# Attention probabilities turned in 32x32 blocks and exchanged between partitions by DMA, with one float32 product per key tile

## The chip, the core and the metric

The kernel runs on one core of one Trainium2 chip. The core has five engines that take their instructions in order and meet at semaphores: TensorE (PE, with its weight loads as PEld), VectorE (DVE), ScalarE (ACT), GpSimd (POOL) and SyncE (SP, which only issues transfers here). A row ending in q (ACTq, SPq) is an instruction of an engine's queue, such as the issue of a transfer. Data lies in SBUF (128 partitions) and in PSUM (8 banks of 2 KB per partition). The metric is the device time of one execution, in microseconds; smaller is better.

## The reference

One gated cross-attention block and one gated feed-forward block, in float32. What the change touches is the attention: 16 heads, 2 batches of 512 query rows, 1024 keys of width 128.

```python
q_big = jnp.einsum('bshk,hkq->bshq', q_hk, w_kc_q)
q_r = jnp.einsum('bshq,hqr->bhsr', q_big, W_qr)
k_r = jnp.einsum('bld,hdr->bhlr', kv_rope, W_kr)
scores = jnp.einsum('bhsr,bhlr->bhsl', q_r, k_r)
attn = jax.nn.softmax(scores, axis=-1)
ctx_c = jnp.einsum('bhsl,bld->bhsd', attn, kv_rope)
...
out = ctx_lat.reshape(b, s, H * K) @ Wo.T
...
x = x + jnp.tanh(g_xattn[0]) * _L0_xattn_ref(...)
x = x + jnp.tanh(g_ffn[0]) * _L0_ffn_ref(...)
```

## The kernel before

**Units.** The heads go in 8 pairs. A pair has 4 units `w` = 0 to 3: batch `w // 2`, and of it one half of the query rows. A unit is 4 score tiles (2 groups of 128 rows times 2 heads) of 128 rows by 1024 keys, so there are 32 units. Pair 0 is written out, pairs 1 to 3 are a loop, pairs 4 to 6 and 7 are written out again. Each unit has 8 steps `c`, one for each tile of 128 keys; tables such as `SCORE_STEP`, `MAX_STEP`, `EXP_STEP` and `SIDE` say at which step each engine does what.

**Softmax of a unit.** `score_matmuls` (L1324) makes 2 tiles in 12 products of float32 split in a high and a low part (`q_hi`, `q_lo`, `k_hi`, `k_lo`), into the 4 banks of `ps_s`. They hold 2 tiles, so each group of 12 waits until the exponentials of the 2 tiles before it are done (`exp_done`). `max_tile` (DVE, L1675) takes the row maximum, `exp_tile` (ACT, L1514) writes the exponentials to `E` with their row sums, `inv_tile` (DVE, L1680) inverts the sums, and `pool_scale` (POOL, L1128) scales the tile in place. All this is done one unit ahead of the unit whose probabilities are used.

**Probabilities times keys.** At each step TensorE turns four 128x128 pieces of `E` against the identity (L1377) into a bank of `ps_b`. ACT rounds the bank to its high part `et_hi` (L1471), DVE subtracts to get the low part `et_lo` (L1636), and `pv_matmuls` adds three products (L1335 to L1337) to `ps_ctx`, some steps behind (`PV_STEP`). When a unit's 8 key tiles are in, `ctx_high` and `ctx_low` split `ps_ctx` for the output products.

**Side tasks.** The `SIDE` table puts other products between these: `m` and `a` (weight products for the next pair, L1255 and L1266), `q` and `k` (next queries and keys, L1297 to L1299 and L1276 to L1278), `b` (L1303) and `out` (L1231 to L1233). ACT makes the high part of `a`, `q`, `k`, `b` (`side_high`) and DVE the low part, or adds an `out` to `x_sb` (`side_low`, L1661). Each result is taken out of its bank one step behind its product. The banks of `ps_b` rotate through turned probabilities and side tasks.

**Feed-forward weights.** During pairs 0 to 3 ACT sums the absolute weights in halves of 1024 columns (`sum_half`, L1528), during pairs 4 to 6 it takes their tanh (`tanh_half`, L1538) and DVE rounds them (`round_half`, L1697). SP loads each half in `sp_pair` (L1100). The feed-forward block starts during the last pair and then has the core to itself.

Of the kernel before, what the change touches and what calls it, by code (L numbers as in the profile page):

```python
# [33 lines left out]
P = 128  # L34
# [38 lines left out]
SUM_STEPS = {0: (5, 7), 1: (5,), 2: (5, 7), 3: (6,)}  # L73
TANH_STEPS = {w: (2, 6) for w in range(4)}
ROUND_STEPS = {w: (5, 7) for w in range(4)}
SUM_HALVES, QUANT_HALVES, SUM_PAIRS = 6, 8, 4
LAST_ROUND_AT = (0, 3)

SIDE = [
# [4 lines left out]
]  # L88
WK_AT = (1, 1)
KV1_AT = (1, 6)  # L90

XN_AT = ((0, 2), (0, 6), (1, 2), (1, 6))

XN_LOW_AT = ((1, 1), (1, 3), (2, 1), (2, 3))
# [3 lines left out]
def side_tasks(w, first, last):  # L98


    def wanted(task):
        before = task[:2] == ("out", 3)
        behind = task[0] in ("m", "a", "k", "q")
        return not (first and before or last and behind)
    early = last and w == 3
    return {c - early: task for c, task in SIDE[w].items() if wanted(task)}
# [50 lines left out]
BANKS = 3  # L157
PLACES = 51


def bank_users(first, last):

    users = []
    for w in range(4):
        side = side_tasks(w, first, last)
        for c in range(LT):
            users.append(("turn", w, c))
            if c in side:
                users.append(side[c])
    return users  # L170


USERS = {v: bank_users(v == "first", v == "last") for v in ("first", "mid", "last")}
PLACE0 = {"first": PLACES - 1 - len(USERS["first"]), "mid": 0, "last": 0}
PLACE = {v: {u: PLACE0[v] + i for i, u in enumerate(us)} for v, us in USERS.items()}
assert len(USERS["mid"]) <= PLACES and USERS["first"][-3:] == USERS["mid"][-3:]


def bank_of(variant, user):
    return PLACE[variant][user] % BANKS  # L180


def bank_before(variant, user):

    at = PLACE[variant][user] - BANKS
    if at < PLACE0[variant]:
        if variant == "first":
            return None, False
        at += PLACES
        mid = USERS["mid"]  # L190
        return (mid[at], True) if at < len(mid) else (None, False)
    return USERS[variant][at - PLACE0[variant]], False

def build(nc, A):
    with ExitStack() as ctx:
# [21 lines left out]
        E = sb("E", [P, 2, ST, LCTX])  # L220
# [44 lines left out]
        wq_s = sa("wq_s", [P, 2, DIM])  # L265
        wkcq_s = sa("wkcq_s", [P, 2, QT, HK])
# [10 lines left out]
        kv_hi = sa("kv_hi", [P, BATCH, LT, DC], F32R)  # L277
        kv_lo = sa("kv_lo", [P, BATCH, LT, DC], F32R)
        et_hi = sa("et_hi", [P, ET_RING, NF], F32R)
        et_lo = sa("et_lo", [P, ET_RING, NF], F32R)  # L280
        ctx_hi = sa("ctx_hi", [P, 2, SEQ], F32R)
        ctx_lo = sa("ctx_lo", [P, 2, SEQ], F32R)
# [3 lines left out]
        wo_s = sa("wo_s", [P, 2, DIM])  # L286
# [31 lines left out]
        g3 = E[:, 0, 0:2, :].rearrange("p a b -> p (a b)")  # L318
# [5 lines left out]
        ps_et, ps_side = ps_b[:, 0:2, :], ps_b[:, 2, :]  # L324
        ps_s4 = ps_s[:, :, :].rearrange("p a (b c) -> p (a b) c", c=NF)
# [7 lines left out]
        xn = E[:, 1, :, :].rearrange("p a b -> p (a b)").rearrange("p (t d) -> p t d", d=DIM)  # L333
# [39 lines left out]
        LAST_SIDE = SIDE_PER_PAIR * 7 + SIDE_BASE + len(ORDER["last"])  # L373


        def rope_parts(eng, b, ls):
# [6 lines left out]
            def table(c, lo, hi):  # L383
# [7 lines left out]
                    lambda: eng.tensor_tensor(kv_raw[:, b, ls, :], kv_raw[:, b, ls, :], rot[:, b, ls, :], ALU.add))  # L391
# [82 lines left out]
        def ffn_sp(sp):  # L474

            sp.wait_ge(et_done, LT * (UNITS - 3) + 1)
# [3 lines left out]
            sp.wait_ge(et_done, LT * (UNITS - 1))  # L480
# [593 lines left out]

        def sp_pair(sp, p, variant, mode):
            if is0(p):
                load_bw(sp, p)
            if variant != "last":

                sp.wait_ge(side_done, 2 if is0(p) else SIDE_PER_PAIR * p + (SIDE_BASE - SIDE_PER_PAIR + ORDER["mid"][("a",)] + 1))  # L1080
                load_q(sp, p + 1)
                load_wq(sp, p + 1)

                sp.wait_ge(wk_ready, p + 1)
                load_kr(sp, p + 1)
            if not is0(p):

                sp.wait_ge(side_done, SIDE_PER_PAIR * p + (SIDE_BASE - SIDE_PER_PAIR + ORDER["mid"][("b", 1)] + 1))
                load_bw(sp, p)
            if mode is None:  # L1090
                return
            if is0(p):
                for ready in (kv0_front, kv0_back, kv1_ready):
                    sp.wait_ge(ready, 1)
            for g in range(SUM_HALVES if mode == "sum" else QUANT_HALVES):
                if not (is0(p) and g < 2):
                    sp.wait_ge(w_taken, halves_before(p, mode) + (g - 1))
                j, half = divmod(g, 2)
                row = p + WPARTS * j if mode == "sum" else WPARTS * p + (j - WPARTS * SUM_PAIRS)
                sp.dma_start(w_stage[:, half, :], A["wffn"][bass.ds(row, 1), :, half * WHALF:(half + 1) * WHALF]  # L1100
                             .rearrange("o p f -> p (o f)")).then_inc(ld_w[half], 16)

        @block.sync
        def _(sp):
# [7 lines left out]
            sp.wait_ge(ld_ctx[1], 16)  # L1112
            sp_pair(sp, 0, "first", "sum")
# [27 lines left out]
        def pool_unit(pool, p, w, last=False):  # L1141

# [743 lines left out]
```

## Time and profile before

| | |
|---|---|
| median of 3 runs | 730.16 us (729.91 to 730.49) |
| span of the profiled execution | 728.8 us |
| median less the span, what lies around the profiled instructions | 1.4 us |
| 32 units of attention, from the first step to the last product on `ps_ctx` | about 37.6 to 635.5 us of the span |
| one pair of heads in the loop | 75.0 us |
| busy in the 75 us from 186 to 261 | PE 75.0, DVE 55.8, ACT 48.6, POOL 18.1 us |
| granted TensorE clock | 1.00 throughout (2.4 GHz) |

The shares of busy time tell which engine has no room left; the start times of neighbouring rows tell how long a step holds an engine, which for TensorE is shorter than the duration of one product, because products overlap. Both are used below.

### The profile page before, as it was taken

The numbers are of one execution on the slowest core, as the hardware profiler recorded it, in microseconds if no ns is written. First come the engines' busy times: TensorE is split into PE (matmuls) and PEld (weight loads), VectorE is DVE, ScalarE is ACT, GpSimd is POOL, SyncE is SP. The second block draws the span as 40 slices with busy tenths as digits, with TensorE's granted clock in tenths as the row PEclk, the third lists the DMA queues.
The fourth block names the chain that finished last, engine by engine and source line by source line (L and its number), as shares of the span: only waits on it lengthen the run. The fifth ranks groups of instructions, "written<-read, shape, count | busy, mean of one in ns | idle before, by whom it ended". The sixth has DMA issues, their size and how long they took to land.

```text
span 728.8 us, 11950 instructions
## 1 busy us (share of the span) xinstructions
PE 714.5 (98%) x4142; PEld 530.5 (73%) x4142; DVE 567.6 (78%) x1016; ACT 486.6 (67%) x821; POOL 253.2 (35%) x235
## 2 busy tenths in 40 slices
PE   9899999999999999999999999999999999999997
PEld 7577788777877787778777877787777776645553
DVE  6778877777787777767878787878887889999873
ACT  3677765666667656666666666666676766478876
POOL 4744422222212222222222223222322334677651
PEclk9999999999999999999999999999999999999999
DMA  8401164114010401040114213543250001000001
GB/s 280 149 31 58 36 240 157 46 34 154 29 58 29 158 29 58 29 158 31 59 58 158 58 59 119 178 151 117 66 191 12 28 2 58 1 1 28 17 30 45
DMA packets 22124, 58.32 MB, mean 80 GB/s; under 512 B 4032, under 2 KB 7232, under 8 KB 21312
## 3 DMA queue, kind: packets, MB, share of 16 engines
q1 hardware_dynamic: 19904, 44.96, 18.5%
q0 software_dynamic: 784, 10.49, 3.8%
q10 hardware_dynamic: 1392, 2.29, 0.9%
q8 instruction: 26, 0.43, 0.2%
q14 instruction: 18, 0.15, 0.1%
HBM read 51.45 MB, written 6.29 MB: 79 GB/s over the span
## 4 chain that ended last, share of the span: by engine, by line
PE 82%; DVE 7%; ACT 3%; POOL 3%; issue 2%; DMA 2%; ACTq 0%; SPq 0%; POOLq 0%; DVEq 0%
PE ps_b L1377 14%; PE ps_s L1324 13%; PE ps_ctx L1335 9%; PE ps_ctx L1337 7%; PE ps_ctx L1336 7%; PE ps_s L587 4%; PE ps_b L1233 4%; PE ps_b L1231 4%; PE ps_b L1232 4%; PE ps_b L1297 2%; PE ps_b L638 2%; PE ps_b L1299 2%; PE ps_b L1298 2%; PE ps_b L1266 2%; PE ps_b L1303 2%
## 5 line engine op out<-in xcount | busy, mean ns | idle before, releaser
L1128 POOL TENSOR_SCALAR E<-E,small 128x1024 f32<-128x1024 f32 x128 | 148.7, 1162 | 413.0 <-DVE small L1680 413.0
L1471 ACT ACTIVATE et_hi<-ps_b 128x512 fp32r<-128x512 f32 x256 | 152.9, 603 | 163.1 <-PE ps_b L1377 163.1
L1636 DVE TENSOR_TENSOR et_lo<-ps_b,et_hi 128x512 fp32r<-128x512 f32 x256 | 175.0, 684 | 43.0 <-ACT et_hi L1471 42.4
L1675 DVE TENSOR_REDUCE small<-ps_s 128x1 f32<-128x1024 f32 x128 | 153.0, 1216 | 4.7 <-PE ps_s L1324 3.0
L1377 PEld LDWEIGHTS ps_b<-ident,E 128*128 128x128 f32 x1024 | 124.7, 140 | 40.6 <-issue 8.8
L1377 PE MATMUL ps_b<-ident,E 128*128 128x128 f32 x1024 | 152.1, 273 | 1.3 <-DVE et_lo L1636 0.8
L1514 ACT ACTIVATE E<-ps_s,small 128x1024 f32<-128x1024 f32 x128 | 142.9, 1117 | 5.7 <-DVE small L1675 5.5
L1335 PE MATMUL ps_ctx<-et_hi,kv_hi 128*128 128x512 f32 x256 | 121.0, 472 | 0.7 <-DVE ctx_lo L1636 0.7
L1337 PE MATMUL ps_ctx<-et_lo,kv_hi 128*128 128x512 f32 x256 | 101.1, 395 | 0.0
L1336 PE MATMUL ps_ctx<-et_hi,kv_lo 128*128 128x512 f32 x256 | 100.5, 393 | 0.0
L1661 DVE SCALAR_TENSOR_TENSOR x_sb<-ps_b,small,x_sb 128x512 f32<-128x512 f32 x62 | 46.2, 746 | 29.3 <-PE ps_b L1233 29.3
L1335 PEld LDWEIGHTS ps_ctx<-et_hi,kv_hi 128*128 128x128 f32 x256 | 48.3, 189 | 25.1 <-issue 15.6
L1324 PE MATMUL ps_s<-k_hi,q_hi 64*128 64x512 f32 x256 | 57.2, 443 | 3.1 <-ACT E L1514 1.5
L587 PE MATMUL ps_s<-wq,q12T 128*128 128x512 fp8e4 x256 | 59.9, 379 | 0.1
L1337 PEld LDWEIGHTS ps_ctx<-et_lo,kv_hi 128*128 128x128 f32 x256 | 48.0, 188 | 11.1
L1324 PE MATMUL ps_s<-k_hi,q_lo 64*128 64x512 f32 x256 | 50.8, 391 | 0.0
L1324 PE MATMUL ps_s<-k_lo,q_hi 64*128 64x512 f32 x256 | 50.6, 390 | 0.0
L1231 PE MATMUL ps_b<-b_hi,ctx_hi 128*128 128x512 f32 x128 | 50.4, 394 | 0.0
L1233 PE MATMUL ps_b<-b_lo,ctx_hi 128*128 128x512 f32 x128 | 50.3, 393 | 0.0
L1336 PEld LDWEIGHTS ps_ctx<-et_hi,kv_lo 128*128 128x128 f32 x256 | 48.8, 191 | 1.5
L1232 PE MATMUL ps_b<-b_hi,ctx_lo 128*128 128x512 f32 x128 | 49.8, 389 | 0.0
L514 POOL TENSOR_TENSOR hg<-h_f,E 128x512 f32<-128x512 f32 x32 | 40.5, 1276 | 21.2 <-DVE h_f L922 21.2
(188 smaller groups left out, 1070.0 us busy)
## 6 DMA issues: line engine op xcount, KB each, us to landing
w_stage<-in_wffn SPq DMA_DIRECT2D x48, 512.0 KB, 3.4
xnT<-xn_split POOLq DMA_DIRECT2D x3, 2048.0 KB, 9.5
wo_s<-in_woT SPq DMA_DIRECT2D x8, 512.0 KB, 6.0
xn_split<-xnT POOLq DMA_DIRECT2D x2, 2048.0 KB, 9.3
wq_s<-in_wq SPq DMA_DIRECT2D x7, 512.0 KB, 5.8
wkcq_s<-in_wkcqT SPq DMA_DIRECT2D x7, 384.0 KB, 4.3
out<-x_sb SPq DMA_DIRECT2D x8, 256.0 KB, 2.0
x_sb<-in_x SPq DMA_DIRECT2D x3, 512.0 KB, 7.3
```

Of the source, the lines that this page charges most:

```text
L587: last = nc.tensor.matmul(ps_s4[:, 2 * i + c % 2, :], q12T[:, k, i, d, :], wq8[:, DT * i + d, cols], start=(d == 0), stop=(d == DT - 1))
L1128: nc.gpsimd.tensor_scalar(e, e, rowinv[:, k:k + 1], 1.0, ALU.mult, ALU.mult).then_inc(scaled, 1)
L1231: nc.tensor.matmul(into, ctx_hi[:, u % 2, cols], b_hi[:, h, :], start=(h == 0), stop=False)
L1324: last = nc.tensor.matmul(ps_s[:, h, cols], q[head, b, rows], k[head, b, cols], start=(i == 0), stop=(i == 2))
L1335: nc.tensor.matmul(ps_ctx[:, :], kv_hi[:, b, c, :], et_hi[:, c % ET_RING, :], start=(c == 0), stop=False)
L1336: nc.tensor.matmul(ps_ctx[:, :], kv_lo[:, b, c, :], et_hi[:, c % ET_RING, :], start=False, stop=False)
L1337: nc.tensor.matmul(ps_ctx[:, :], kv_hi[:, b, c, :], et_lo[:, c % ET_RING, :], start=False, stop=(c == LT - 1))\
L1377: last = nc.tensor.transpose(into[:, s * P:(s + 1) * P], E[:, w % 2, s, c * P:(c + 1) * P], ident[:, :])
L1471: return nc.scalar.activation(out, in_, ACT.Copy)
L1514: nc.scalar.activation(E[:, w % 2, t, :], ps_s[:, t % 2, :], ACT.Exp, bias=negmax[:, k:k + 1], accum_out=rowsum[:, k:k + 1]).then_inc(exp_ ...
L1636: return nc.vector.tensor_tensor(out, full, hi.bitcast(F32), ALU.subtract)
L1675: nc.vector.tensor_reduce(negmax[:, k:k + 1], ps_s[:, t % 2, :], AX_X, ALU.max, negate=True).then_inc(max_done, 1)
```

## The change

The turn of the probabilities leaves TensorE. `E` is laid out as partition, parity of the unit, key quarter, tile, 256 keys. After scaling, DVE turns each tile in place in 32x32 blocks (`turn_blocks`, 4 instructions a unit). Then 16 transfers of 32 partitions x 4 KB a unit move partition quarter `i` of `E` to quarter `g` of a new tensor `G` (`exchange`): SP issues quarters 0 and 1, ACT quarters 2 and 3, 8 transfers each. The copies `et_hi`, `et_lo`, `kv_hi`, `kv_lo` are gone, and each key tile takes one product of unsplit float32 operands, `kv` and `G`. Softmax runs two units ahead in place of one (`AHEAD = 2`), `ps_ctx` and the third bank of `ps_b` take turns as the sum of a unit, and the side tasks take turns in the other two banks. SP's loads are mixed with its exchanges. The tables of steps change accordingly.

```diff
+AHEAD = 2
+SCORE_STEP = {0: 0, 4: 1}
+MAX_STEP = {1: (0, 1), 5: (2, 3)}
+EXP_STEP = {1: 0, 2: 1, 5: 2, 6: 3}
+INV_STEP = {3: 0, 4: 1, 6: 2, 7: 3}
+TURN_OWN = {4: 0, 5: 1}
+TURN_NEXT = (2, 3)
+CTX_HIGH_STEP, CTX_LOW_STEP = 0, 1
+EXCHANGE_ACT_STEP = 1
...
+        SP_QUARTERS, ACT_QUARTERS = (0, 1), (2, 3)
...
+        def exchange(eng, passed, p, w, quarters):
+            par = w % 2
+            eng.wait_ge(blocks_turned, 16 * p + (4 * w + 4))
+            eng.sem_inc(passed, 1)
+            if not (is0(p) and w < 2):
+                eng.wait_ge(pv_done, 4 * p + (w - 1))
+            for i in quarters:
+                for g in range(4):
+                    eng.dma_start(G[g * QUAD:(g + 1) * QUAD, par, i, :, :], E[i * QUAD:(i + 1) * QUAD, par, g, :, :])\
+                        .then_inc(exchanged[par], 16)
...
+        def pv_matmul(pe, p, w, c):
+            if c == 0:
+                pe.wait_ge(exchanged[w % 2], 2 * EXCHANGE * p + EXCHANGE * (w // 2 + 1))
+                if not (is0(p) and w < 2):
+                    pe.wait_ge(ctx_done, 4 * p + (w - 1))
+            turned = G[:, w % 2, :, :, key_tile(c)].rearrange("p i t q -> p t i q")
+            last = nc.tensor.matmul(CTX_PS[w % 2].rearrange("p (t i q) -> p t i q", t=ST, i=4), kv[:, w // 2, c, :], turned,
+                                    start=(c == 0), stop=(c == LT - 1))
...
+        def turn_blocks(dve, p, w, t):
+            dve.wait_ge(scaled, 16 * p + (4 * w + t + 1))
+            nc.vector.transpose(e_tile(w % 2, t), e_tile(w % 2, t)).then_inc(blocks_turned, 1)
...
-                    act.wait_ge(et_done, 32 * p + (8 * w + c + 1))
-                    copy_act(et_hi[:, c % ET_RING, :], ps_b[:, bank_of(variant, ("turn", w, c)), :]).then_inc(ethi_done, 1)
-                    if c in EXP_STEP and not (variant == "last" and w == 3):
-                        exp_tile(act, *next_unit(p, w), EXP_STEP[c])
+                        side_high(act, p, variant, task, ps_b[:, side_bank(variant, task), :])
+                    if c in EXP_STEP and not (variant == "last" and w >= AHEAD):
+                        exp_tile(act, *unit_ahead(p, w, AHEAD), EXP_STEP[c])
+                    if c == EXCHANGE_ACT_STEP and not (variant == "last" and w == 3):
+                        exchange(act, act_passed, *unit_ahead(p, w, 1), ACT_QUARTERS)
```

ACT, the first steps of unit 0 of a loop pair, before. `et_hi` is the high part of a turned key tile, `E` gets the exponentials of a tile.

```order
L1471 ACTIVATE et_hi<-ps_b 128x512 [waits et_done]
L1512 ISA
L1514 ACTIVATE E,small<-ps_s,small 128x1024 [waits max_done]
L1552 REGISTER_ALU
L1471 ACTIVATE et_hi<-ps_b 128x512 [waits et_done]
L1512 REGISTER_ALU
L1514 ACTIVATE E,small<-ps_s,small 128x1024 [waits max_done]
L1518 ISA
L1471 ACTIVATE ctx_hi<-ps_ctx 128x512 [waits pv_done]
```

ACT, unit 1 of a loop pair, changed.

```order
L1446 ACTIVATE ctx_hi<-ps_ctx 128x512 [waits pv_done]
L1451 REGISTER_ALU
L1446 ACTIVATE b_hi<-ps_b 128x512 [waits side_done]
L1451 REGISTER_ALU
L1446 ACTIVATE k_hi<-ps_b 128x512 [waits side_done]
L1479 REGISTER_ALU
L1483 ACTIVATE E,small<-ps_s,small 128x2x4x128 [waits exchanged1,max_done]
L1055 DMA G<-E 32x1024 [waits blocks_turned,pv_done]
L1055 DMA G<-E 32x1024 x7
L1451 REGISTER_ALU
L1446 ACTIVATE k_hi<-ps_b 128x512 [waits side_done]
L1483 ACTIVATE E,small<-ps_s,small 128x2x4x128 [waits max_done]
```

Eight issues of the exchange now stand between the first exponential of a unit and the second, and in unit 1 also ahead of the second `k_hi`; before, a copy of 128x512 stood there.

DVE, the start of the same unit, changed.

```order
L1653 STREAM_TRANSPOSE E<-E 128x4x256 [waits scaled] x2
L1614 REGISTER_ALU
L1608 TENSOR_TENSOR b_lo<-ps_b,b_hi 128x512 [waits side_hi]
L1656 ISA
L1608 TENSOR_TENSOR ctx_lo<-ps_ctx,ctx_hi 128x512 [waits ctxhi_done]
L1614 REGISTER_ALU
L1608 TENSOR_TENSOR k_lo<-ps_b,k_hi 128x512 [waits side_hi]
L1641 REGISTER_ALU
L1643 TENSOR_REDUCE small<-ps_s 128x1 [waits scores_done]
L1641 REGISTER_ALU
L1643 TENSOR_REDUCE small<-ps_s 128x1 [waits scores_done]
```

The first maximum of a unit comes behind two block turns, `ctx_lo` and the low part of the side task of step 0.

PE, from step 3 to step 4 of unit 1, changed.

```order
L1333 MATMUL ps_b<-G,kv 128x512
L1340 REGISTER_ALU
L1228 MATMUL ps_b<-b_hi,ctx_hi 128x512 [waits ctx_done,side_freed]
L1229 MATMUL ps_b<-b_hi,ctx_lo 128x512
L1230 MATMUL ps_b<-b_lo,ctx_hi 128x512
L1228 MATMUL ps_b<-b_hi,ctx_hi 128x512
L1229 MATMUL ps_b<-b_hi,ctx_lo 128x512
L1230 MATMUL ps_b<-b_lo,ctx_hi 128x512
L1313 REGISTER_ALU
L1321 MATMUL ps_s<-k_hi,q_hi 128x512 [waits exp_done]
```

The second group of scores of a unit stands behind the `out` of step 3, whose wait on `side_freed` is for the side task two places back, in unit 1 the second `k`; it waits itself for the second exponential of the same unit. Before, a unit's two groups stood at steps 7 and 3, among key tiles of four transposes each.

## Rows read from the trace of the kernel before

**Rows 1.** The page: busy time, and slices of the span with the clock.

```profile
PE 714.5 (98%) x4142; PEld 530.5 (73%) x4142; DVE 567.6 (78%) x1016; ACT 486.6 (67%) x821; POOL 253.2 (35%) x235
...
PEclk9999999999999999999999999999999999999999
```

**Rows 2.** Stretches: length, PE, PEld, DVE, ACT, POOL busy, clock, DMA, GB/s.

```profile
37.00:111.00 74.00, 72.75 (x427) 55.88 (x424) 56.10 (x89) 52.51 (x94) 29.65 (x22) 1.00 0.27 93
186.00:261.00 75.00, 75.00 (x439) 58.99 (x438) 55.77 (x89) 48.58 (x90) 18.07 (x16) 1.00 0.21 67
562.00:638.00 76.00, 72.49 (x409) 53.07 (x408) 68.36 (x154) 48.68 (x82) 33.38 (x34) 1.00 0.06 21
```

**Rows 3.** PE in time: start us, us, what; one key tile.

```profile
331.72 0.60 PE L1377 MATMUL ps_b<-ident,E 128*128 128x128 f32 x4
332.07 0.48 PE L1335 MATMUL ps_ctx<-et_hi,kv_hi 128*128 128x512 f32 x1
332.38 0.40 PE L1336 MATMUL ps_ctx<-et_hi,kv_lo 128*128 128x512 f32 x1
332.62 0.39 PE L1337 MATMUL ps_ctx<-et_lo,kv_hi 128*128 128x512 f32 x1
332.85 0.60 PE L1377 MATMUL ps_b<-ident,E 128*128 128x128 f32 x4
```

**Rows 4.** PE in time: a float32 product of 512 columns, in two records.

```profile
50.07 1.02 PE L1303 MATMUL ps_b<-wo_s,wkv_s 128*128 128x512 f32 x2
50.92 0.60 PE L1377 MATMUL ps_b<-ident,E 128*128 128x128 f32 x4
```

**Rows 5.** All engines in time: one group of 12 score products, and the maxima behind it.

```profile
313.88 0.50 PE L1324 MATMUL ps_s<-k_hi,q_hi 64*128 64x512 f32 x2
...
315.47 0.50 PE L1335 MATMUL ps_ctx<-et_hi,kv_hi 128*128 128x512 f32 x1
315.57 2.36 DVE L1675 TENSOR_REDUCE small<-ps_s 128x1 f32<-128x1024 f32 x2 [0.27 <-PE ps_s L1324]
```

**Rows 6.** Groups: line, engine, what, count, busy us, mean ns, idle before.

```profile
L1636 DVE TENSOR_TENSOR et_lo<-ps_b,et_hi 128x512 fp32r<-128x512 f32 x256 | 175.0, 684 | 43.0 <-ACT et_hi L1471 42.4
L1675 DVE TENSOR_REDUCE small<-ps_s 128x1 f32<-128x1024 f32 x128 | 153.0, 1216 | 4.7 <-PE ps_s L1324 3.0
L1471 ACT ACTIVATE et_hi<-ps_b 128x512 fp32r<-128x512 f32 x256 | 152.9, 603 | 163.1 <-PE ps_b L1377 163.1
L1514 ACT ACTIVATE E<-ps_s,small 128x1024 f32<-128x1024 f32 x128 | 142.9, 1117 | 5.7 <-DVE small L1675 5.5
L1128 POOL TENSOR_SCALAR E<-E,small 128x1024 f32<-128x1024 f32 x128 | 148.7, 1162 | 413.0 <-DVE small L1680 413.0
L1697 DVE TENSOR_SCALAR wq<-w_stage 128x1024 fp8e4<-128x1024 f32 x24 | 16.3, 678 | 0.0
L390 POOL TENSOR_TENSOR wq<-wq,w_stage 128x1024 f32<-128x1024 f32 x1 | 2.1, 2138 | 0.0
```

**Rows 7.** ACT's queue in time: the transfers that it issues at the start.

```profile
1.68 0.45 ACTq L1062 DMA_DIRECT2D wkcq_s<-in_wkcqT  x1
2.16 0.45 ACTq L1063 DMA_DIRECT2D wqr_s<-in_wqr  x1
2.64 1.24 ACTq L1069 DMA_DIRECT2D wkr_s<-in_wkr  x1
3.92 0.50 ACTq L1058 DMA_DIRECT2D x_sb<-in_x  x1
```

**Rows 8.** Transfers: what, issuer, count, KB each, us from issue to landing.

```profile
w_stage<-in_wffn SPq DMA_DIRECT2D x48, 512.0 KB, 3.4
xn_split<-xnT POOLq DMA_DIRECT2D x2, 2048.0 KB, 9.3
```

**Rows 9.** PE in time: the longest wait of the prologue.

```profile
19.83 0.51 PE L1324 MATMUL ps_s<-k_hi,q_hi 64*128 64x512 f32 x2 [1.51 <-DVE q_lo L1636]
```

More of the change, by code:

```diff
@@ L104, in wanted @@
         return not (first and before or last and behind)
-    early = last and w == 3
-    return {c - early: task for c, task in SIDE[w].items() if wanted(task)}
+    return {c: task for c, task in SIDE[w].items() if wanted(task)}
 PROLOGUE_TASKS = [("m",), ("a",), ("k", 0, 0), ("k", 0, 1), ("q", 0, 0), ("q", 0, 1), ("k", 1, 0), ("k", 1, 1), ("q", 1)]
@@ L152, in hi_index, with side_bank @@
     return HI_PER_PAIR * p + (HI_BASE + HI_ORDER[variant][task])
[L157 to L192, printed above, removed]
+def side_bank(variant, task):
+    return (SIDE_BASE + ORDER[variant][task]) % 2
+assert SIDE_PER_PAIR % 2 == 0
 def build(nc, A):
@@ L265, in build @@
         wq_s = sa("wq_s", [P, 2, DIM])
+        with ExitStack() as place:
+            wo_s = place.enter_context(nc.sbuf_tensor("wo_s", [P, 2, DIM], F32))
         wkcq_s = sa("wkcq_s", [P, 2, QT, HK])
@@ L1173, in pool_pair @@
                     load_xn(pool, p, 0)
+                if last and w == 2:
+                    rms_root(pool, 0)
+                    pool.wait_ge(ld_g, 32)
+                    normed(pool, -2, 0)
+                    normed(pool, -1, 1)
+                    ln2_root(pool, 1)
+                    rms_root(pool, 1)
         @block.gpsimd
@@ L1215, in _ @@
             normed_row(7)
-            for t in range(ST):
-                pool_scale(pool, 0, 0, t)
+            for w in range(AHEAD):
+                for t in range(ST):
+                    pool_scale(pool, 0, w, t)
             pool_pair(pool, 0)
@@ L1375, in pe_pair @@
-                    into = ps_b[:, bank_of(variant, ("turn", w, c)), :]
-                    for s in range(ST):
-                        last = nc.tensor.transpose(into[:, s * P:(s + 1) * P],
-                                                   E[:, w % 2, s, c * P:(c + 1) * P], ident[:, :])
-                    last.then_inc(et_done, 1)
-                    ahead, half = SCORE_STEP.get(c, (4, 0))
-                    if w + ahead < (4 if variant == "last" else 6) and ahead < 4:
-                        if (w + ahead, half) == (2, 0) and not is0(p):
+                        pe.wait_ge(xnt_copied, TT)
@@ L1387, in pe_pair @@
-                    for back, tile in PV_STEP[c]:
-                        if not (variant == "first" and w < back):
-                            pv_matmuls(pe, *((p, w - back) if w >= back else (p - 1, 3)), tile)
+                        score_matmuls(pe, *unit_ahead(p, w, AHEAD), SCORE_STEP[c])
+                    pv_matmul(pe, p, w, c)
                     if c in tasks:
                         wait_bank(pe, p, variant, tasks[c])
-                        side_matmuls(pe, p, variant, tasks[c], ps_b[:, bank_of(variant, tasks[c]), :])
+                        if mean and tasks[c] == ("out", 3, 0):
+                            pe.wait_ge(mean_chain, 1)
+                        side_matmuls(pe, p, variant, tasks[c], ps_b[:, side_bank(variant, tasks[c]), :])
@@ L1464, in _ @@
             pe_pair(pe, 7, "last")
-            for back, tile in PV_STEP[0] + PV_STEP[1]:
-                pv_matmuls(pe, 7, 3, tile)
             ffn_pe(pe)
```

352 lines of the change are left out of this document (166 added, 186 removed), and 7 rows, old and new, of the table SIDE.

## The prediction

> **What bounds the kernel now.** The page's first section comes first: TensorE is busy for 714.5 of 728.8 us, with its clock at the full level in every slice [rows 1]. The stretches show the same inside the loop: 75.0 of 75 us on PE, 55.8 on DVE, 48.6 on ACT, 18.1 on POOL [rows 2]. So the loop runs at TensorE's pace, and what takes time off TensorE pays only until something else is late. Durations of single products overlap, so I count by start times. A key tile costs four transposes 0.35 us (331.72 to 332.07) and three products 0.78 us (to 332.85), together 1.13 us [rows 3]. A group of 12 score products holds PE for 1.59 us (313.88 to 315.47), and the maxima start 1.69 us after its start [rows 5]. By the 0.23 us step of split products [rows 3] the six of an `out` take 1.4 us and the twelve of a `q` 2.8 us. A pair then is 32 x 1.13 = 36.2 us of key tiles and 36.9 us of scores and side tasks, 73.1 against the 75.0 measured; the 2 us missing are small gaps, and I add them to each pair below.
>
> **What TensorE gains.** The float32 product that takes the place of seven instructions is in the trace: it holds PE from 50.07 to 50.92, 0.85 us [rows 4]. That is 0.28 us less a tile, 9 us a pair: 64.1 + 2 = 66 us of TensorE work. The trace shows no product whose moving operand comes in runs of 32 numbers; I take the dense price, since nothing here points to another, with 0.78 us (three split steps) below and twice 0.85 above.
>
> **What the others gain and get.** ACT loses 256 copies of 0.60 us, DVE 256 subtractions of 0.68 us [rows 6], 4.8 and 5.5 us a unit. DVE gets four block turns of 128x1024 a unit. None is in the trace; the nearest rows of that size are the rounding (0.68 us, SBUF to SBUF), the maximum (1.22 us) and POOL's product of two operands (2.14 us) [rows 6]. I take 1.2, the row of DVE that moves one number a lane in a step, with 0.68 and 2.14 for the range. DVE's sum stays near 53 us a pair, ACT's falls to 29 us, and ACT gets the exchange.
>
> **The issue of the exchange.** ACT issues 8 transfers a unit. Its issues at the start lie 0.48 us apart (1.68, 2.16, 2.64), and the fifth of the burst holds the queue 1.24 us, so that the next starts at 3.92 [rows 7]. Eight are 3.84 us at the usual step, 4.6 with one such hold. An issue doesn't need ACT's arithmetic, so it can lie beside the exponential before it (1.12 us [rows 6]); nothing in the rows shows whether it does. Ends: 2.7 us (full overlap) and 4.6 (none, one hold). I take 3.9 us counted from the end of the first maximum, that is overlap and no hold. Landing isn't late: 2048 KB land in 9.3 us in one transfer [rows 8], and the products on `G` come more than 12 us after the issue.
>
> **Why this lies on the path.** The order of ACT in a unit is `ctx_hi`, high parts, exponential 0, eight issues, exponential 1. TensorE's second group of scores (step 4) waits for exponential 1 of the same unit, since `ps_s` holds two tiles; behind it are queued four key tiles, the side tasks and the next unit. Before, ACT had a 0.6 us copy there, and waited for TensorE in total 163 us over 256 copies [rows 6]: that slack is gone. So I follow the chain through a unit, in two parts.
>
> Part A, from the start of the first group of scores to the start of the second. At the start DVE still owes work of the last unit: inverse of the last exponential, POOL's scaling (1.16 us and 0.2 to start), block turn, so that it is free about 3.9 us in (4.7 after unit 0). Then come `ctx_lo` (0.7), the low part of step 0's side task, maximum 0 (1.2), issues (3.9), exponential 1 (1.2).
> - Unit 0: 3.9 + 0.7 = 4.6, the `m` copies 5.0, maximum to 6.2, issues to 10.1, exponential to 11.3: 11.4 us.
> - Unit 1: DVE free at 4.7, `b_lo` 5.3, `ctx_lo` 6.0, `k_lo` 6.7, maximum 7.9, issues 11.8. Now ACT's second `k_hi` (12.4) and DVE's second `k_lo` (13.1) come, for which the `out` of step 3 waits; `out` 1.4: 14.5 us.
> - Unit 2: `k_lo` 4.8, maximum 6.0, issues 9.9, exponential 11.1: 11.2 us.
> - Unit 3: scores 1.6 + product 0.9 + `q` 2.9 = 5.4, its high and low parts 6.7, maximum 7.9, issues 11.8, exponential 13.0: 13.1 us.
>
> TensorE's own work in part A is 8.4, 8.7, 8.5 and 10.4 us, so it waits 2.7 to 5.8 us in each unit. Sum of A: 50.2 us.
>
> Part B, from the second group to the next unit, ends with the last exponential or with TensorE's work, whichever is later. In unit 3 it is 1.7 (scores) + 1.2 + 1.2 (maxima) + 1.2 (exponential) = 5.4 us. Unit 2 has a `k_hi` ahead of the last exponential: 6.1. Unit 1 has `q_hi` there, whose products end at 6.3: 8.1. In unit 0 `a` ends at 4.4, `a_hi` 5.0, `a_lo` 5.7, two maxima 8.1, exponential behind `b_hi`: 10.1. Sum of B: 29.7 us.
>
> A pair: 50.2 + 29.7 + 2 = 82 us against 75.0, so **the path gets 7 us longer while TensorE has 9 us less to do**.
>
> **The sum.** Prologue: softmax of units 0 and 1 now comes before the first product on keys. TensorE's last prologue task ended at 36.0; two groups of scores with their maxima and exponentials put its end near 43.8, ACT's `q_hi` at 45.4, eight issues 49.3, landing 2 us more (512 KB land in 3.4 [rows 8]): first product at 51.3, first unit from 49.7 (before 37.6). Pair 0 has four more ACT copies of 1.1 us, one of them on the path: +1.5. Seven pairs: 7 x 82 = 574. Rounding in pairs 4 to 6 stands ahead of DVE's turns: +1.5. Pair 7 has scores in two units only: 17.7 + 17.1, then 16 products, four `out` and the first feed-forward work, 28.6 us (unit 3 can't start before its exchange, issued 3.9 us into unit 2, has landed, about 11 us in): 63.4 against 73. The feed-forward rest is as before: 728.8 - 635.5 = 93.3. Together 49.7 + 1.5 + 574 + 1.5 + 63.4 + 93.3 = 783.4 of span, and with the 1.4 us around it **785 us**, 7.5% slower. Of the ends: issues at 2.7 take 1.2 us off each of 30 units (750), at 4.6 they add 21 (806); turns at 0.68 take off about 0.9 us a unit (758), at 2.14 they add about 2.6 (860).
>
> **Rival 1, faster: the issues don't hold ACT's arithmetic.** If exponential 1 starts while the issues run, part A is 8.5, 12.0, 8.6, 10.4, a pair 39.5 + 29.7 + 2 = 71 us, and the sum 46 + 1.5 + 497 + 1.5 + 57 + 93.3 + 1.4 = 698 us. It decides at about 0.15 us of ACT's time an issue, where a pair would be 75 again. Against it stand 0.43 to 0.50 us a row [rows 7]; for it only that no row here has an ACT instruction queued behind an issue, apart from the very start. The Trainium skill speaks for it: "Advanced Engine Details and Errata", section "Sequencer Loop", says that further engine instructions can be read and queued while a control instruction is being executed. If a DMA issue is such an instruction, that gives the 698 us; no row here shows it either way. Chance 0.17, with the shades between (700 to 728).
>
> **Rival 2, slower: TensorE's clock falls in the new waits.** The longest wait of PE in the trace is 1.5 us [rows 9], at clock 1.00; the new ones reach 5.8 us in unit 1. If the clock drops to 1.2 GHz there, the `out` and the scores behind it take double: 3 us more a pair on the path, 805 us. The Trainium skill ("TensorE: Matmul & The Clock Gate", "What's actually happening") says that the array goes to the lower clock when it has idled; here no run shows it. Chance 0.2.
>
> **Rival 3, slower by more: the turn costs 2 us, or ACT's issues back up** while SP's eight are still being moved: 830 to 870 us. The share of busy time of the DMA engines, 0.21 to 0.27 [rows 2], is low, but a unit now adds 2 MB in 20 us, 100 GB/s to the 67. Chance 0.08.
>
> **Rival 4: no difference.** The issue term and TensorE's gain would have to cancel within 1.5 us. Chance 0.03.
>
> **How the numbers follow.** Forecast 785 us, chance 0.52. A measurement of this kernel can tell 0.2%. Slower: 0.52 + 0.2 + 0.08 = 0.80; same 0.03; faster 0.17. To hold 8 in 10 the range leaves out rival 1's lower part and the far end of rival 3: 722 to 850 us. The forecast's own range is 750 to 815.
>
> **What would show each step.** In the profile of the changed kernel: the product on `G` starts 0.85 us apart from its neighbour; a block turn lasts 0.7 to 1.3 us; in ACT's timeline eight issues 0.45 to 0.5 us apart between two exponentials; among PE's waits, scores waiting for ACT's `E` and `out` waiting for DVE's `k_lo`, together some 10 to 15 us a pair; `m` products 82 us apart; PE's busy share near 80% in the loop. The prediction is wrong if exponential 1 starts within 1.5 us of exponential 0, or if the second group of scores doesn't wait.

## The result, and the profile after

The changed kernel takes 896.0 us (893.7 to 898.5 over 4 runs) against 730.2 us, a ratio of 1.227 with a 95% interval of 1.2256 to 1.2285. The forecast was 785 us with a range up to 850: the direction was right, the size was not.

The page of the changed kernel, parts 1, 2, 4, 5 and 6; part 5 has line, engine, what, count, busy us, mean ns, and the idle time before with what ended it:

```profile
PE 713.5 (80%) x2862; PEld 414.4 (46%) x2862; DVE 553.8 (62%) x886; ACT 358.6 (40%) x563; POOL 254.2 (29%) x235
PEclk9968898989889888999988988888898998899999
PE 40%; DVE 22%; ACTq 19%; issue 8%; ACT 6%; DMA 3%; POOL 2%; DVEq 0%; SPq 0%; POOLq 0%
L1653 DVE STREAM_TRANSPOSE E<-E 128x1024 f32<-128x1024 f32 x128 | 154.1, 1224 | 20.0 <-POOL E L1122 16.6
G<-E SPq DMA_DIRECT2D x256, 128.0 KB, 3.2
G<-E ACTq DMA_DIRECT2D x256, 128.0 KB, 4.7
```

Against [rows 1], PE is busy for 80% of the span instead of 98%, and its clock, at the full level in every slice before, stands below it in many slices of the loop. In the chain of work that ended last, ACTq has 19%: ScalarE's queue, issuing transfers. Before, the same line of the page had it at 0%:

```profile
PE 82%; DVE 7%; ACT 3%; POOL 3%; issue 2%; DMA 2%; ACTq 0%; SPq 0%; POOLq 0%; DVEq 0%
```

The waits of PE in the changed kernel say for what it stands idle (waited for, us in total, times, longest):

```profile
PE ps_s L1321 <- ACT E L1483: 113.3, 39, 7.2
PE ps_b L1228 <- DVE k_lo L1608: 36.4, 7, 5.4
PE ps_ctx L1333 <- DMA G<-E: 7.6, 1, 7.6
```

The 113.3 us are the wait of the second group of scores for exponential 1. Why that exponential is late stands in ScalarE's own timeline, here in unit 3 of pair 2, whose first group of scores started at 320.04 (start us, us, engine, what, idle before):

```profile
325.56 0.60 ACT L1446 ACTIVATE q_hi<-ps_b 128x512 fp32r<-128x512 f32 x1 [4.95 <-PE ps_b L1296]
328.05 1.11 ACT L1483 ACTIVATE E<-ps_s,small 128x1024 f32<-128x1024 f32 x1 [1.89 <-DVE small L1643]
328.21 1.27 ACTq L1055 DMA_DIRECT2D G<-E  x2
329.51 4.24 ACTq L1055 DMA_DIRECT2D G<-E  x6
333.86 1.11 ACT L1483 ACTIVATE E<-ps_s,small 128x1024 f32<-128x1024 f32 x1 [4.61 <-issue]
```

The issues begin 0.16 us after exponential 0 has begun, so an issue does lie beside an arithmetic instruction ahead of it. Exponential 1 starts 0.1 us after the last issue has ended, so it doesn't lie beside one behind it. The eight take 5.5 us, where ScalarE idles 4.61. All issues of `G<-E` in the trace (count; duration in ns, least, median, most):

```profile
L1055 SPq DMA_DIRECT2D G<-E x256: 507/592/1857, 40.4 to 773.8; - x128
L1055 ACTq DMA_DIRECT2D G<-E x256: 514/618/2203, 44.7 to 774.4; - x128
```

The second half of the loss is in PE's timeline behind that wait (unit 2 of pair 2):

```profile
311.76 0.80 PE L1321 MATMUL ps_s<-k_hi,q_hi 64*128 64x512 f32 x2 [3.93 <-ACT E L1483]
312.35 0.63 PE L1321 MATMUL ps_s<-k_lo,q_hi 64*128 64x512 f32 x2
312.78 0.63 PE L1321 MATMUL ps_s<-k_hi,q_lo 64*128 64x512 f32 x2
...
314.06 0.63 PE L1321 MATMUL ps_s<-k_hi,q_lo 64*128 64x512 f32 x2
314.62 2.95 PE L1333 MATMUL ps_ctx<-G,kv 128*128 128x512 f32 x4
317.00 0.79 PE L1273 MATMUL ps_b<-kvT_hi,wk_hi 128*128 128x512 f32 x1
```

After 3.93 us of idling the score products step by 0.43 us, not 0.23 as in [rows 5]: the group takes 2.86 us instead of 1.59, and the two key tiles behind it 2.38. Two tiles at the full level, earlier in the same unit:

```profile
302.33 1.88 PE L1333 MATMUL ps_ctx<-G,kv 128*128 128x512 f32 x4
303.64 0.80 PE L1228 MATMUL ps_b<-b_hi,ctx_hi 128*128 128x512 f32 x1
304.28 0.39 PE L1229 MATMUL ps_b<-b_hi,ctx_lo 128*128 128x512 f32 x1
```

These take 1.31 us. The granted clock of the two stretches (columns as in [rows 2]) says why:

```profile
302.33:304.28 1.95, 1.95 (x7) 0.94 (x5) 1.73 (x4) 0.60 (x1) 0.00 (x0) 1.00 0.30 67
311.76:314.62 2.86, 2.86 (x13) 1.83 (x13) 1.28 (x2) 2.13 (x4) 1.12 (x1) 0.50 0.49 123
```

It is 1.00 in the first and 0.50 in the second: the group of scores behind the wait runs at the lower of the two levels, 1.2 GHz.

Below I use the prediction's two parts of a unit, summed over the four units of a pair: **A** from the first group of scores to the second, **B** from there to the next unit. Each is a difference of start times of L1321 in the trace. Of pair 2: A 57.6 (13.1, 16.7, 12.7, 15.1) and B 38.0 (12.4, 9.6, 8.3, 7.7), together 95.6 us. Predicted: 50.2, 29.7 and 2 of small gaps.

### The profile page after: what moved, and what is told of

It is laid out like the page before. It is cut to its first block, busy times and chain, and to the rows that moved or that the text cites. A ratio compares the mean times of both kernels' runs of the same rounds, so it can differ in the third digit from the quotient of the medians.

```text
span 891.8 us, 9351 instructions
## 1 busy us (share of the span) xinstructions
PE 713.5 (80%) x2862; PEld 414.4 (46%) x2862; DVE 553.8 (62%) x886; ACT 358.6 (40%) x563; POOL 254.2 (29%) x235
## 4 chain that ended last, share of the span: by engine, by line
PE 40%; DVE 22%; ACTq 19%; issue 8%; ACT 6%; DMA 3%; POOL 2%; DVEq 0%; SPq 0%; POOLq 0%
ACTq L1055 19%; PE ps_s L1321 13%; DVE small L1643 7%; PE ps_b L1333 6%; PE ps_ctx L1333 5%; DVE E L1653 5%; PE ps_s L557 3%; ACT E L1483 3%; DVE wq L1670 2%; PE ps_b L1263 2%; DMA G<-E 2%; PE ps_b L608 2%; DVE k_lo L1608 1%; PE ps_b L1296 1%; PE ps_b L1294 1%
## 5 line engine op out<-in xcount | busy, mean ns | idle before, releaser
L1653 DVE STREAM_TRANSPOSE E<-E 128x1024 f32<-128x1024 f32 x128 | 154.1, 1224 | 20.0 <-POOL E L1122 16.6
L1321 PE MATMUL ps_s<-k_hi,q_hi 64*128 64x512 f32 x256 | 71.2, 548 | 117.6 <-ACT E L1483 113.3
L1333 PE MATMUL ps_ctx<-G,kv 128*128 128x512 f32 x256 | 138.7, 654 | 7.6 <-DMA G<-E 7.6
L1333 PE MATMUL ps_b<-G,kv 128*128 128x512 f32 x256 | 133.0, 634 | 0.2 <-DMA G<-E 0.2
L1228 PE MATMUL ps_b<-b_hi,ctx_hi 128*128 128x512 f32 x128 | 76.1, 594 | 40.5 <-DVE k_lo L1608 36.4
L1321 PEld LDWEIGHTS ps_s<-k_hi,q_hi 64*128 64x128 f32 x256 | 30.7, 232 | 161.2 <-ACT E L1483 136.4
L1648 DVE RECIPROCAL small<-small 128x1 f32<-128x1 f32 x128 | 19.2, 154 | 87.6 <-ACT E L1483 87.1
L1333 PEld LDWEIGHTS ps_ctx<-G,kv 128*128 128x128 f32 x256 | 48.8, 207 | 53.1 <-issue 42.2
L1333 PEld LDWEIGHTS ps_b<-G,kv 128*128 128x128 f32 x256 | 49.0, 203 | 46.3 <-issue 41.6
L1321 PE MATMUL ps_s<-k_hi,q_lo 64*128 64x512 f32 x256 | 64.3, 492 | 0.0
L1321 PE MATMUL ps_s<-k_lo,q_hi 64*128 64x512 f32 x256 | 64.0, 490 | 0.0
L1228 PEld LDWEIGHTS ps_b<-b_hi,ctx_hi 128*128 128x128 f32 x128 | 25.9, 202 | 65.4 <-DVE k_lo L1608 43.2
L1608 DVE TENSOR_TENSOR k_lo<-ps_b,k_hi 128x512 fp32r<-128x512 f32 x31 | 21.0, 681 | 39.9 <-ACT k_hi L1446 39.9
## 6 DMA issues: line engine op xcount, KB each, us to landing
xnT<-xn_split POOLq DMA_DIRECT2D x3, 2048.0 KB, 13.1
```

The costliest lines, as they stand in the source:

```text
L1228: nc.tensor.matmul(into, ctx_hi[:, cols], b_hi[:, h, :], start=(h == 0), stop=False)
L1321: last = nc.tensor.matmul(ps_s[:, h, cols], q[head, b, rows], k[head, b, cols], start=(i == 0), stop=(i == 2))
L1333: last = nc.tensor.matmul(CTX_PS[w % 2].rearrange("p (t i q) -> p t i q", t=ST, i=4), kv[:, w // 2, c, :], turned, start=(c == 0), stop=(c ...
L1653: nc.vector.transpose(e_tile(w % 2, t), e_tile(w % 2, t)).then_inc(blocks_turned, 1)
```

## The experiments

All runs are edits of the changed kernel. The first three take ScalarE's issues away, move them or double them, two fill PE's wait, and one halves ScalarE's issues at their place; the others look for a better version.

**All 16 issues on SyncE**

```
-        SP_QUARTERS, ACT_QUARTERS = (0, 1), (2, 3)
+        SP_QUARTERS, ACT_QUARTERS = (0, 1, 2, 3), ()
```

> SyncE issues all 16 transfers of a unit, ScalarE none; its waits before them stay. Theory (the issues hold ScalarE's arithmetic, 5.1 to 7.4 us a unit between exponential 0 and exponential 1, 30 units): about 165 us less, 731 us (715 to 755), pair near 73 us, the second group of scores waits under 1 us, and SyncE's issues take 0.5 to 0.6 us each beside other work. Rival A (what is late is VectorE's chain or the landing, and the issues lie in its shadow): above 870 us. Rival B (SyncE's 16 issues, 10 us, then delay the landing so that the first product on G waits): 760 to 800 us with a wait of PE on DMA G<-E of 1 to 3 us in each unit.

Measured: 731.1 us (727.4 to 734.2), the kernel before within error (ratio 1.0012, 0.9986 to 1.0038). Its page, PE's waits, its issues, and the stretch 194 to 264 us, which is pair 2 (length, PE, PEld, DVE, ACT, POOL busy, clock, DMA share, GB/s):

```profile
PE 657.4 (90%) x2862; PEld 383.1 (53%) x2862; DVE 548.7 (75%) x886; ACT 355.1 (49%) x563; POOL 254.2 (35%) x235
PE ps_b L1333 <- DMA G<-E: 21.6, 6, 7.1
PE ps_s L1321 <- ACT E L1483: 16.1, 23, 2.3
L1055 SPq DMA_DIRECT2D G<-E x512: 507/592/1988, 40.7 to 613.3; - x171
194.00:264.00 70.00, 67.19 (x278) 39.94 (x280) 52.55 (x75) 32.72 (x61) 18.03 (x17) 1.00 0.76 196
```

Pair 2 is 69.5 us: A 39.6, B 29.9. The wait for exponential 1 is all but gone, and with it the low clock: the clock is 1.00 in that stretch, and B falls by 8.1 us although nothing in it was changed. That the total met the forecast so well is partly luck: a steady pair gained 26 us where I had reckoned 22, and pairs 5 and 6 (78.3 and 84.0 us) lost part of it to a new wait on the landing of `G`. The median issue is 592 ns here too, with ScalarE issuing nothing, so SyncE's price isn't made by two engines issuing at once.

**ScalarE's issues behind exponential 1**

```
-EXCHANGE_ACT_STEP = 1
+EXCHANGE_ACT_STEP = 2
```

> ScalarE's eight issues stand behind exponential 1 instead of ahead of it. Theory (an issue costs ScalarE's time wherever it stands, and what counts is who waits behind it): the second scores start 5.5 us sooner, then exponential 2 can begin 2.9 us after exponential 1 but finds the issues until 5.5 us: 2.6 us given back, 3 us a unit gained, 800 us (785 to 825). If the issues cost nothing: 896 us. If exponential 2 has slack of its own: 740 us.

Measured: 795.1 us (two runs, 791.3 and 798.8), pair 2 81.6 us (A 45.1, B 36.5). The same eight issues cost 100 us less at a place where less stands behind them; what is left is that the sum and tanh of `w_stage` now wait for them, with exponential 2 behind:

```profile
ACT w_stage L1497 <- issue: 62.9, 14, 5.6
ACT w_stage L1507 <- issue: 60.4, 12, 8.7
```

**Twice as many issues for the same bytes**

```
-                    eng.dma_start(G[g * QUAD:(g + 1) * QUAD, par, i, :, :], E[i * QUAD:(i + 1) * QUAD, par, g, :, :])\
-                        .then_inc(exchanged[par], 16)
+                    for n in range(0, QUAD, QUAD // 2):
+                        to, at = g * QUAD + n, i * QUAD + n
+                        eng.dma_start(G[to:to + QUAD // 2, par, i, :, :], E[at:at + QUAD // 2, par, g, :, :])\
+                            .then_inc(exchanged[par], 16)
```

> Each transfer cut into two of 16 partitions, so 16 issues of 64 KB a unit on ScalarE and 16 on SyncE, same bytes. If an issue costs by the instruction (0.62 us): 8 more a unit on the path, 5 us x 30 = 150 us more, 1046 us. If it costs by its bytes or rows: 0.3 us each, 896 us within 15. If the price has a fixed and a row part: between, which gives both parts.

Measured: 1049.6 us. In pair 2 A is 76.4 and B 36.3: 32 more issues on ScalarE made A 18.8 us longer, 0.59 us each. The issues of this run:

```profile
L1057 ACTq DMA_DIRECT2D G<-E x512: 514/612/2422, 44.4 to 928.2; - x171
```

Half the rows and bytes, the same 0.6 us: the price is by the issue.

**Spare products in the wait.** Behind exponential 0 and ahead of the wait for exponential 1, 14 products whose result is overwritten:

```
+                if s == 1:
+                    pe.wait_ge(exp_done, 16 * p + (4 * w + 1))
+                    for _ in range(FILL):
+                        nc.tensor.matmul(ps_s[:, 0, 0:NF], q_hi[:, 0, 0:P], k_hi[:, 0, 0:NF], start=True, stop=True)
                 pe.wait_ge(exp_done, 16 * p + (4 * w + 2 * s))
```

> 14 spare products (0.23 us each at 2.4 GHz, results overwritten) stand behind exponential 0 and ahead of the wait for exponential 1, so TensorE idles less before the second group of scores. Clock theory (this wait lets the clock fall to 1.2 GHz, and the group of scores then takes 2.86 us instead of 1.59 and the key tile behind it double): granted clock above 0.95 and 1.5 to 2 us less a unit, 840 to 860 us. Rival (the clock's loss lies beside other work): 890 to 900 us. If the spare products end after exponential 1, up to 0.5 us a unit more.

Measured: 893.9 us (two runs, 891.1 and 896.8), which by the total alone would have favoured the rival. The parts say otherwise. B of pair 2 is 29.65 us (10.06, 8.22, 6.04, 5.33), as without the issues; but A of unit 1 is 21.1 us instead of 16.7, because there PE is late itself (it waited for `k_lo`) and the spare products came on top. So the fill was left out there and in the prologue (`if s == 1 and w != 3`, and none for the units of the prologue):

> As the run before with 14 spare products, but only in the units where TensorE is early: not for unit 3's scores (step 4 of unit 1, where they lengthened the stretch from 16.7 to 21 us) and not in the prologue. Clock theory: the stretch from the second group of scores to the next unit shrinks by 2.2 to 2.4 us in three units of four (12.4 to 10.1, 8.3 to 6.0, 7.7 to 5.3), the stretch ahead of it grows by 0.3 to 0.5 us: 5.6 us a pair less, pair 90 us, 855 us in all (850 to 868). Rival (the clock's loss lies beside work of VectorE and ScalarE that is as late): 890 to 900 us.

Measured: 867.4 us (866.6 to 871.7), 28.6 less than the change with more work on TensorE. Pair 2: A 57.9, B 30.9, 88.8 us instead of 95.6. PE's timeline there, the spare products in the first row:

```profile
297.32 3.35 PE L1316 MATMUL ps_s<-k_hi,q_hi 128*128 128x512 f32 x14
301.93 0.50 PE L1325 MATMUL ps_s<-k_hi,q_hi 64*128 64x512 f32 x2 [1.26 <-ACT E L1487]
302.26 0.40 PE L1325 MATMUL ps_s<-k_lo,q_hi 64*128 64x512 f32 x2
302.50 0.40 PE L1325 MATMUL ps_s<-k_hi,q_lo 64*128 64x512 f32 x2
```

After a wait of 1.26 us the step is 0.23 us again. In pair 2, A, the issues' part, hasn't moved; B, the clock's part, has given back 7.1 of its 8.3 us. Over the seven pairs, B falls from 255.0 to 222.6 us while A goes from 421.5 to 427.7. I had expected 855 us: pair 6 gained 0.6 us instead of 5.6, and what follows it about 1. In pair 6 there was less to gain and not all of it came: B was 34.5 us there without the fill (the clock had stayed up behind one of its waits) and 35.0 with it, and behind the spare products of its unit 2 a wait of 3.28 us was left, after which the group of scores took the slow step again (B of that unit 8.7 us instead of 6.05).

**Four issues at the place of the change**, SyncE 12 (`SP_QUARTERS, ACT_QUARTERS = (0, 1, 2), (3,)`):

> SyncE issues 12, ScalarE 4 at the place of the change (between exponential 0 and exponential 1). By the sum (maximum 0 ends, 2.5 us of issues from then, exponential 1.2) the first stretch of the four units is 9.9, 13.1, 9.7 and 11.6 us against 8.7, 10.8, 8.7 and 10.8 of TensorE's own: 5.3 us a pair more than with none, 750 us (740 to 765). If only a burst that fills the queue costs and four issues are free: as the run with four late.

Measured: 775.4 us. In pair 2 A is 46.8 (10.2, 13.6, 10.1, 13.0), 2.5 us over the sum, and pairs 5 and 6 took 82.3 and 87.2 us. By the number of ScalarE's issues a unit, A of pair 2 is:

| issues on ScalarE | 0 | 4 | 8 | 16 |
|---|---|---|---|---|
| A, us | 39.6 | 46.8 | 57.6 | 76.4 |

From 4 to 8 it is 0.68 us an issue, from 8 to 16 0.59. At 0 PE's own work sets A. This run also has its share of the low clock: in pair 1 a wait of 2.39 us was enough for the group of scores behind it to take the slow step.

The other runs look for a version that beats both kernels. First **SyncE 12, ScalarE 4 behind exponential 1** (both edits above):

> SyncE issues 12 transfers, ScalarE 4, behind exponential 1, where 2.9 us pass before exponential 2 can start. Theory (four issues of 0.62 us fit in that gap, and the exchange is issued 2.4 us sooner than by SyncE alone): no cost on ScalarE, and most of the 29 us that the products on G waited in the run with SyncE alone are gone: 708 us (700 to 722), faster than the kernel before. Rival (an issue behind which an exponential stands costs wherever it is): 760 us. Rival (the late exchanges of pairs 4 to 6 are held by the transfers in flight, not by the issuing engine): 725 to 731 us.

Measured: 729.9 us, ratio 0.9987 (0.9965 to 1.0009). The four issues are nearly free: a steady pair is 70.1 us, 0.6 more than with none on ScalarE and 5 less than before. But the second rival was right on the rest: pairs 5 and 6 took 80.7 and 86.0 us. Two stretches of pair 5, the transfers that fall into them, and the wait at their end:

```profile
450.00:460.00 10.00, 8.92 (x41) 4.86 (x39) 9.26 (x14) 6.58 (x11) 4.66 (x4) 1.00 1.09 291
460.00:470.00 10.00, 3.71 (x7) 2.29 (x8) 2.35 (x3) 0.00 (x0) 0.48 (x1) 0.61 1.03 247
445.20 0.59 POOL L1143 DMA_DIRECT2D xnT<-xn_split  x1
446.64 11.21 SPq L1055 DMA_DIRECT2D G<-E  x12
466.29 2.08 PE L1333 MATMUL ps_b<-G,kv 128*128 128x512 f32 x2 [6.95 <-DMA G<-E]
```

The DMA engines are fully busy (share 1.09 and 1.03) while 2048 KB of `xnT` come in; SyncE's twelve issues take 11.2 us, where twelve medians of 0.59 are 7.1, and the products on `G` start 8.4 us after the last of them has ended (457.85 to 466.29). Most other bursts of twelve in this run took 8 to 9 us. The longest, 12.3 us, was in pair 6.

**SyncE's loads of `w_stage` behind the exchange** (the loop over `stage_load` moved below it, with 12 and 4 issues):

> As the run with 12 and 4 issues, and SyncE's loads of w_stage stand behind the exchange of their unit instead of ahead of it. If the loads (they wait for VectorE's rounding, and bring 1 MB just ahead of the exchange) are what makes the exchange late in pairs 4 to 6: 8 to 15 us less than that run. If they are not: the same within 3 us; if the loads then come too late for their tanh at step 3: up to 15 us more.

Measured: 896.2 us, 166 more than with the loads ahead, where the worst I allowed was 15. ScalarE's sum and tanh then stand in its queue until the load lands, with the exponentials behind them:

```profile
ACT w_stage L1497 <- DMA w_stage<-in_wffn: 127.7, 18, 13.8
ACT w_stage L1507 <- DMA w_stage<-in_wffn: 116.8, 17, 14.2
```

**The reloads of `xnT` 10 us later** (`load_xn` behind the second `pool_scale` of the next unit):

> As the run with 12 issues on SyncE and 4 late ones on ScalarE; GpSimd's three 2048 KB reloads of the normed activations (pairs 5 and 6) stand behind the second scaling of the next unit, some 10 us later, so behind that unit's exchange instead of in its midst. Theory (three times these 2 MB share the DMA engines, at a busy share of 1.0 to 1.1, with the exchange: 10, 7.5 and 10 us of wait): two thirds of the 27 us go, 712 us (705 to 722). Rival (the reload then collides with the following exchange and holds the queries' products as long): 725 to 735 us.

**The same, with 8 and 8 issues**, ScalarE's in two fours (`{0: (2,), 2: (3,)}` by step):

> As the run before it, but SyncE and ScalarE issue 8 each: ScalarE's in two fours, one ahead of exponential 0 (it waits there some 2.3 us for maximum 0 in any case), one behind exponential 1. Theory (issues cost only where an arithmetic instruction is ready behind them): at most 0.3 us a unit from the fours, against 2.4 us earlier landing: within 5 us of the run before, best case 5 us less. Rival (the fours ahead of exponential 0 hold the high parts or exponential 0 by 1 us or more in each unit): 25 us more. Both use the same number of issues as the change, at other places.

Measured: 729.5 us (ratio 0.9995, 0.9978 to 1.0013) and 767.3 us. Moving the reloads took 2 and 4 us off pairs 5 and 6 (78.6, 81.7), not 18 together, as the rival said: waits of PE for `G` of 5.2, 3.9 and 4.8 us are left in these pairs, the first and the last of them 11 us behind the issue of a reload. The two fours cost 5.8 us a steady pair (75.9), which was that run's rival, 38 us in all where it said 25: the four ahead of exponential 0 aren't free. They stand behind `ctx_hi` and ahead of a `k_hi`, for whose low part an `out` on PE waits. Nor is it only the issues that hold ScalarE there: it also has to stand at the exchange's own wait for VectorE's block turns. In unit 2 of pair 2 `ctx_hi` ended at 257.3, VectorE's turns at 260.1, and the four issues ran from 260.2 to 262.6, so that `k_hi` came 5.5 us behind `ctx_hi`, 2.5 of them issues. These waits in ScalarE's list:

```profile
ACT k_hi L1445 <- issue: 56.3, 10, 6.4
```

**GpSimd issues four** ahead of its scalings, SyncE 8, ScalarE 4 late; and **8 and 8 only in pairs 5 and 6**:

> SyncE issues 8, GpSimd 4 (ahead of its scalings, where it waits some 5 us for the inverse in any case), ScalarE 4 behind exponential 1; reloads later as in the run before the last. Theory (issues cost only where arithmetic is ready behind them, and no queue holds more than 8): steady pair 70 us as before, the exchange issued in 5 us instead of 7.4, so less of the late landing of pairs 5 and 6 (78.6 and 81.7 us a pair with 12 on SyncE) and of the prologue: 718 us (710 to 727). Rival A (GpSimd's issues take over 1 us each, or its queue is behind a reload of 2048 KB): 735 to 750. Rival B (the landing in pairs 5 and 6 is bound by bytes): 727 to 730.

> 12 on SyncE and 4 late on ScalarE in pairs 0 to 4, but 8 and 8 (two fours) in pairs 5 and 6, where the run with 8 and 8 had 78.3 and 77.8 us a pair against 78.6 and 81.7; prologue 8 and 8. Theory (the two add up): 729.5 - 4.2 - 2 for the prologue = 723 us (719 to 728). Rival (what 8 and 8 had there comes from its slower pairs ahead): 729 to 732.

Measured: 730.7 us (ratio 1.0001, 0.9981 to 1.0021) and 729.6 us (0.9993, 0.9983 to 1.0003). Both miss the forecast gain. GpSimd's issues are cheap, and no scaling stands among what waits for them:

```profile
L1060 POOL DMA_DIRECT2D G<-E x128 | 64.0, 505 | 62.1 <-issue 45.6 <-DVE E L1663 16.4
```

Yet all these versions end at 730 us, as if tied. They aren't: by the trace of the version with GpSimd, a steady pair is 5 us shorter than before, and pair 7 some 7 us, but the first unit starts 9.6 us later (softmax of two units stands ahead of it instead of one), pair 0 is 4 us longer than 75 and pairs 5 and 6 are 2 and 3 us longer, and what follows pair 7 takes 2 us more. In pairs 5 and 6 PE waits 4.3 and 3.7 us there for the reload of `xnT` itself, and 2.6 us for `G`. So this version gives back at the start and around the reloads what it gains in the middle. No version here beats the kernel before by more than the measurement can tell.

## Why the prediction was off

**Right.** The key tile: two tiles of `G` and the first split product behind them go from 302.33 to 304.28, and less 0.23 for that product it is 0.86 us a tile, where 0.85 was taken. The block turn: 1.22 us against 1.2. The issues do overlap the exponential ahead of them, as taken. Which waits appear and where: scores for exponential 1 and `out` for `k_lo`, and beside the first landing of `G` no others of size. And the sum of B, 29.7 us, which the runs without issues (29.9) or with the first fill (29.65) measured.

**Wrong, first: the size of the issue term.** The step says "3.9 us counted from the end of the first maximum". In unit 3, all the rest of its line holds: `q` ends 5.5 us in, the maximum 8.0 (predicted 7.9), but the issues end at 13.7, not 11.8. The 0.48 us was read from issues at the start that load from HBM [rows 7]; these, from SBUF to SBUF, have a median of 0.62 on ScalarE and 0.59 on SyncE (also when SyncE issues alone), with 32 rows or 16. In the same trace SyncE's loads of `wkv_s` and `wo_s` have medians of 0.38 and 0.47. With the longer ones among them a burst is 5.0 to 7.4 us. That is most of A: 57.6 instead of 50.2 in pair 2, 7.4 us (1.4 of them are the clock's, see below). Over the seven pairs A is 421.5 us where the sum had 351.4, 70 us of the missing 111; 19 of these are in pair 0, whose first unit waited for the exchange to land and ran at the low clock. All these bursts are outside even my end of 4.6 us. The only ground for 0.48 was the spacing of those few issues; no row showed an issue of this form at all.

**Wrong, second: rival 2 wasn't a rival but the second half of the answer.** It was priced at 3 us a pair with a chance of 0.2, on the ground that only unit 1's wait of 5.8 us would do it. The forecast itself had waits of 2.7 us and more in each unit, and in the trace waits of 3.1 to 6.3 us stand in units 0, 2 and 3 of pairs 1 to 6, and B is longer than at the full level behind 17 of these 18; in unit 1 the wait for `k_lo` does the same, and there the six products of the `out` behind it take 2.85 us instead of the 1.4 of the sum, which falls into A. So B is 38.0 instead of 29.7 in pair 2, 8.3 us, and over the seven pairs 255.0 instead of 207.9, 47 us. From this go off the 2 us a pair that I added for small gaps (14) and the 3 us added for pair 0 and for rounding, since A and B as measured contain them. The Trainium skill ("TensorE: Matmul & The Clock Gate", "What's actually happening") says that the array drops to the lower clock when it has idled; the trace agrees, 0.43 against 0.23 us a step and a granted clock of 0.50 against 1.00. The mechanism of the forecast and that of rival 2 share their cause, the longer wait, so they could not be alternatives.

**The rest.** The first product on `G` started at 57.12 instead of 51.3: the issues ended at 50.0, near the 49.3 of the sum, but the last landing took 7 us more instead of 2, beside two loads of `w_stage`. Pair 7 took 73.3 us instead of 63.4, since it has the same waits; the end 95.3 instead of 93.3. With pair 0 (105.2 us, A of its unit 0 24.3) this closes the sum: start 46.75, seven pairs 676.4, pair 7 73.3, rest 95.3, together 891.8 us of span.

**Rival 1** fell in the changed kernel: exponential 1 never started beside the issues. The Trainium skill ("Advanced Engine Details and Errata", "Sequencer Loop") says that further engine instructions can be read and queued while a control instruction is being executed. Whether they may also start then, and whether the issue of a transfer is such an instruction, that sentence leaves open; for eight issues the trace shows that exponential 1 started only behind the last, with ScalarE idle 4.61 us ahead of it. It isn't the wait against a register's value in the loop either, since in pair 4, which is written out and waits for constants, it is the same:

```profile
521.35 1.11 ACT L1483 ACTIVATE E<-ps_s,small 128x1024 f32<-128x1024 f32 x1 [4.04 <-issue]
```

But the rival's arithmetic was good: with no issue on ScalarE a pair is 69.5 us where it said 71. Its 698 us were missed by that run because pairs 0, 5 and 6 were longer (519.5 us for seven pairs instead of 500), and pair 7 with the end took 161.7 us instead of 150.3. **Rival 3** was nearest in height, 830 to 870, by reasons that hardly came: the turn isn't 2 us, and ScalarE's bursts of eight were clearly longer than the rest (6.5 to 7.4 us instead of 5.0 to 6.2) only four times, each within 5 us of the issue of a transfer of 2048 KB.

## What to carry to other kernels

Transfers of this form, issued by an engine that also computes, cost it about 0.6 us each, and that delay falls on what stands behind them in its program: count them like instructions, at the price of their own form, and put them where the next arithmetic instruction isn't ready yet. A wait of some microseconds that you put into TensorE's path (here 3.1 to 6.3 us, once 2.39) can have a second price, the products behind it at half speed, so price both together. And read a total only with its parts: the first fill left the total unchanged while it removed one loss and added another.

## What the hardware showed that I had not expected

- An issue of an SBUF-to-SBUF transfer of 128 KB takes 0.59 (SyncE), 0.62 (ScalarE) and 0.50 us (GpSimd), and one of 64 KB on ScalarE 0.61; with the DMA engines' share at 1.0 or above, twelve of them took 11.2 us, where twelve medians are 7.1.
- The lower clock came behind 17 of 18 waits of 3.1 to 6.3 us. Behind one of 3.60 us (unit 3 of pair 6, B 5.4 us) it didn't, nor behind the waits of 0.6 to 1.26 us in pair 2 of the second run with spare products; in the run with four issues at the place of the change it came behind one of 2.39 us. In two of the 17 (waits of 3.82 and 4.00 us in pair 3) the group of scores still took the full step and the clock fell behind it, to a granted 0.84 and 0.72 in the rest of B.
- The moving operand in runs of 32 numbers costs nothing that can be seen: 0.86 us a tile against 0.85 for a dense product.
